# VectorE's running maximum and exponents of the last chunk, put ahead of the second residual and norm of chunk 1

## The reference, cut to what matters

```
def step(carry, kv):                      # time mixing, over 1024 positions
    num, den, mx = carry
    ck, cv = kv
    max_out = jnp.maximum(mx, ck + tf)
    e1 = jnp.exp(mx - max_out)
    e2 = jnp.exp(ck + tf - max_out)
    out = (e1 * num + e2 * cv) / (e1 * den + e2)
    max_st = jnp.maximum(mx + td, ck)
    e1s = jnp.exp(mx + td - max_st)
    e2s = jnp.exp(ck - max_st)
    return ((e1s * num + e2s * cv, e1s * den + e2s, max_st), out)
...
x = _layernorm(x + _L0_attn_ref(x, ...))      # first residual and norm
x = _layernorm(x + _L0_ffn_ref(x, ...))       # second residual and norm
x = _layernorm(x + _L1_attn_ref(x, ...))      # convolutions, gate
x = _layernorm(x + _L1_ffn_ref(x, ...))       # experts
```

## Time and profile before

| | |
|---|---|
| median of 3 runs | 439.88 us (439.57 to 440.08) |
| the profiled execution | 439.91 us, of which its span is 437.8 us |
| TensorE busy | 409.0 us (93% of the span) |
| VectorE busy | 329.8 us (75%) |
| ScalarE busy | 194.4 us (44%) |
| GpSimd busy | 34.1 us (8%) |
| mean granted clock of TensorE | 0.986 of full speed |

### The profile page before, as it was taken

One profiled execution on the slowest core, in us unless ns is written; L12 is line 12 of the kernel. 1 busy time (PEld: TensorE's weight loads), 2 busy tenths in 40 slices (PEclk: granted clock), 3 DMA queues, 4 the chain that ended last, 5 costly groups with the idle time before them and its releaser, 6 DMA issues.

```text
span 437.8 us, 4421 instructions
## 1 busy us (share of the span) xinstructions
PE 409.0 (93%) x1507; PEld 213.3 (49%) x1507; DVE 329.8 (75%) x673; ACT 194.4 (44%) x321; POOL 34.1 (8%) x48
## 2 busy tenths in 40 slices
PE   8776997989999999999999999999999999999994
PEld 3333576668956384354544443334534433443362
DVE  4899998799855995979988798697635861364475
ACT  2355667643165413546155446263054626334432
POOL 1222433111000000000000000000000000000002
PEclk9999898999999999999999999999999999999997
DMA  7300000030000000000000000000000000000001
GB/s 243 129 1 1 1 0 1 15 141 1 0 1 0 2 0 0 1 0 1 1 1 0 0 1 24 1 0 1 0 0 1 25 1 0 1 0 0 1 0 48
DMA packets 4886, 7.10 MB, mean 16 GB/s; under 512 B 1031, under 2 KB 3713, under 8 KB 4737
## 3 DMA queue, kind: packets, MB, share of 16 engines
q1 hardware_dynamic: 4031, 4.92, 3.3%
q10 hardware_dynamic: 834, 1.91, 1.2%
HBM read 5.78 MB, written 1.05 MB: 16 GB/s over the span
## 4 chain that ended last, share of the span: by engine, by line
PE 67%; DVE 23%; ACT 4%; issue 2%; DMA 1%; POOL 1%; SPq 0%; POOLq 0%; DVEq 0%; ACTq 0%
PE ring L1369 22%; PE ring L1349 7%; PE bankA L198 5%; PE ring L1364 4%; PE ring L1351 3%; PE ring L1377 2%; DVE e2v L953 2%; PE ring L1391 2%; PE ring L1384 2%; PE ring L1395 2%; PE bankA L202 2%; PE bankA L300 2%; PE timebank L300 2%; PE specbank L275 2%; PE ring L1388 2%
## 5 line engine op out<-in xcount | busy, mean ns | idle before, releaser
L1369 PE MATMUL ring<-hm,wc 128*128 128x512 f32 (+1 forms) x252 | 108.6, 580 | 0.0
L1369 PEld LDWEIGHTS ring<-hm,wc 128*128 128x128 f32 x252 | 46.1, 190 | 61.0 <-issue 52.1
L1578 DVE SCALAR_TENSOR_TENSOR hm<-xtm,cst,h 128x512 f32<-128x512 bf16 x48 | 33.2, 746 | 2.8 <-ACT h L1483 2.8
L198 PE MATMUL bankA<-wconv,h2w 128*128 128x256 f32 x128 | 32.2, 398 | 0.0
L1497 ACT ACTIVATE gts<-ring 128x512 f32<-128x512 f32 (+1 forms) x18 | 9.9, 550 | 49.0 <-PE ring L1369 49.0
L1483 ACT ACTIVATE h<-ring,vec 128x512 f32<-128x512 f32 x32 | 21.8, 687 | 18.2 <-PE ring L1351 15.7
L198 PEld LDWEIGHTS bankA<-wconv,h2w 128*128 128x128 f32 x128 | 24.0, 197 | 4.7 <-issue 1.8
L1364 PE MATMUL ring<-hm,wc 64*128 64x512 f32 (+1 forms) x84 | 22.9, 621 | 1.3 <-DVE hm L1578 1.3
L1667 DVE SCALAR_TENSOR_TENSOR f2e<-hl,f2e 128x512 f32<-128x512 f32 (+1 forms) x9 | 5.7, 632 | 24.0 <-ACT hl L1528 23.9
L1349 PE MATMUL ring<-zs,wc 128*128 128x512 f32 x40 | 20.8, 603 | 0.8 <-DVE zs L1669 0.8
L1494 ACT ACT_TABLE_LOAD x8 | 10.3, 1283 | 25.3 <-PE ring L1369 25.3
(11 more groups left out here) (280 smaller groups left out, 810.4 us busy)
## 6 DMA issues: line engine op xcount, KB each, us to landing
wc<-in_w_c SPq DMA_DIRECT2D x1, 1664.0 KB
out<-xall SPq DMA_DIRECT2D x8, 128.0 KB, 1.9
cst<-in_const ACTq DMA_DIRECT2D x1, 838.5 KB, 8.9
wc<-in_x_feat SPq DMA_DIRECT2D x1, 768.0 KB, 9.6
wc<-in_k_time ACTq DMA_DIRECT2D x1, 512.0 KB
bconv<-in_bcast SPq DMA_DIRECT2D x1, 512.0 KB, 10.3
wc<-in_x_feat ACTq DMA_DIRECT2D x1, 256.0 KB, 3.8
wa<-in_w_a SPq DMA_DIRECT2D x1, 256.0 KB, 3.7
```

The lines of the kernel that those rows point to most:

```text
L198: ins = pe.matmul(at, h2w[:, n, u % 2, u // 2:u // 2 + P], wconv[:, tap, :], start=False, stop=(h == HALVES - 1 and tap == TAPS - 1))
L1369: ins = pe.matmul(dst[:, at], wc[:, w:w + P], hm[:, seat(j, made + g - 1), at], start=False, stop=(g == PAIRS - 1))
L1578: dve.scalar_tensor_tensor(hm[:, seat(j, k), :], picked, cst[:, C_EG + g:C_EG + g + 1], h[:, g, :], ALU.is_equal, ALU.mult).then_inc(S["hm ...
```

## The change

In VectorE's function `one(c)` the call of `maxima(3)` is taken away from the start of iteration 3 and put into iteration 2, behind `output_end(2)` and ahead of `residual_end(1)`. The condition is written as `c == 2` on the iteration before. All other iterations and all other engines keep their instructions and their order, and no instruction is added or dropped.

```
                 def one(c):
-                    if valid(c):
+                    if valid(c) and not (lambda c: c == 2)(c - 1):
                         maxima(c)
                     if valid(c - 1):
                         residual_mid(c - 1)
...
                         output(c)
                         rounded(c - 1)
                         output_end(c)
+                        if c == 2:
+                            maxima(c + 1)
                         residual_end(c - 1)
```

## The result

The changed kernel takes 443.54 us (median of 16 runs, 442.75 to 445.0), the kernel before 440.38 us (median of 16 runs, 439.37 to 442.91). The ratio is 1.0070, with a 95% interval of 1.0057 to 1.0082: slower by 3.2 us between the medians. Forecast were 441.5 us and a range of 440.4 to 442.9. The direction is right, the size is half of what it should be, and the range doesn't hold it. The three runs known at the time of the prediction had a median of 439.88 us, 0.5 us lower than the later, larger sample.

A forecast was written before the change was run, and what follows sets the result against it. The prediction took ScalarE's queue to set the time between 60 and 70 us. The profiled 439.91 us plus 1.58 gave 441.49, with the median of runs 0.03 lower, so 441.5 us; range 440.4 to 442.9.

The forecast's parts named there:

- The place and the mechanism: Between 60 and 70 us ScalarE's queue sets the time; L605 waits for GpSimd's factors; earlier exponents gain nothing.
- The reason given: ScalarE takes its queue in order with L605 ahead of L629, so exponents ready at 64.3 can't be used sooner.
- The slack of 1.00 us: Chunk 1's norm factors could come 1.00 us later before L605 moved: 66.84 - 65.84.
- GpSimd's factors, 1.29 us taken between 1.29 and 2.13: GpSimd's power and product beside residual_mid(2) were bounded at 1.29 to 2.13 us; the lower end was taken.
- The direct delay of 1.58 us: L605 starts 1.58 us later: 3.35 of delay, less 1.00 of slack, less 0.77 that GpSimd saves.
- nothing absorbs it: TensorE's restart and chunk 3's VectorE chain both move by 1.58 us, and all that follows keeps its distances.
- VectorE's chain had no cover to give: Spare time lies on VectorE, not TensorE: its next statistics wait 1.91 us for TensorE at 86.07.
- The clock, put into the sum at no change: TensorE's 3.41 us at half clock behind its restart stays whole after the change, adding nothing to the sum.
- The prediction's own sign: Much less or more than 3.4 us at 0.50 in the 10 us behind TensorE's restart would show it wrong.
- It costs 3.41 / 2 = 1.7 us now: The half-clock stretch from 73.60 to 77.01, filled with matmuls, costs the kernel before 1.7 us.
- the dearer side: TensorE's low clock lasts longer or a second stretch follows its restart, costing up to another 1.7 us.
- Rival 3: TensorE's longer pause brings more low clock: 0.5 to 1.7 us on top, 442.0 to 443.2 us; chance 0.17.

The follow-up runs named there:

- late_2pow: Kernel before, with two spare GpSimd powers of 128x4 ahead of the factors of chunk 1's second norm: 443.14 us, ratio 1.0055.
- exps_first: Changed kernel, with ScalarE doing chunk 3's three exponentials (L629, L633, L635) ahead of the norm L605 in iteration 3: 441.41 us, ratio 1.0019.
- split_exps: Changed kernel, with ScalarE doing L629 ahead of L605 and L633 and L635 behind the copies h2T and h2w: 440.51 us, ratio 1.0000.
- pad_1op: Kernel before, with one spare VectorE addition of 128x512 ahead of residual_end(1): 440.76 us, ratio 1.0014.
- half_scans: Kernel before, with only the two scans L930 of maxima(3) moved ahead of residual_end(1): 440.96 us, ratio 1.0011.
- late_1pow: Kernel before, with one spare GpSimd power ahead of the factors of chunk 1's second norm: 441.32 us, ratio 1.0013.
- filled kernel of before: Kernel before, with 19 spare matmuls in TensorE's pauses of iterations 3 and 4: 440.0 us, ratio 0.9985.
- filled pair: Kernel before and changed kernel, each with the same 19 spare matmuls in iterations 3 and 4: 440.0 and 441.92 us.
- fill3_after: Changed kernel, with 14 spare matmuls in iteration 3 alone: 442.53 us, ratio 1.0042 to the kernel before.
- fill4_after: Changed kernel, with 5 spare matmuls in iteration 4 alone: 442.92 us, ratio 1.0053 to the kernel before.

## Why the prediction was wrong

- **The place and the mechanism: right.** ScalarE's queue sets the time there, L605 waits for GpSimd, and the exponents that came 2.65 us sooner were of no use behind it. late_2pow shows the cause without VectorE's move. The reason given, that L605 stands ahead of the exponentials, is true but not the whole: with the exponentials ahead (exps_first, split_exps) ScalarE took L629 at 6.54 us behind `rwkv` at the soonest, and in the kernel before the exponents were ready at 6.03.
- **The slack of 1.00 us: right.** Factors that were 0.60, 1.12, 1.26 and 2.34 us late (pad_1op, half_scans, late_1pow, late_2pow) moved L605 by 0.01, 0.11, 0.26 and 1.34 us.
- **GpSimd's factors, 1.29 us taken between 1.29 and 2.13: right.** 67.98 to 69.27 is 1.29. The power beside VectorE's statistics out of PSUM, which the trace of before didn't show, took 1.02 us. The rule of the Trainium skill (SBUF — State Buffer, "Who interferes with whom"), that a VectorE instruction with at most one SBUF input doesn't contend with GpSimd, agrees.
- **The direct delay of 1.58 us, and that nothing absorbs it: right.** 1.58 at L605, 1.58 at TensorE's restart, 1.60 over the loop at full clock, and 313.2 us behind it in both. VectorE's chain had no cover to give, as the prediction says, but also no distance: at full clock it is TensorE that waits for it (0.54 us for `xq` in the filled kernel of before).
- **The clock, put into the sum at no change: the step that failed.** The prediction took the one low stretch behind the restart of the profiled execution as the kernel's own, at a fixed place, and asked only whether that one would move or a second follow. It stands elsewhere from one execution to the next, and there is a second pause, in iteration 4, that the prediction never looked at; the profiled execution of before happened to show nothing behind it. The prediction's own sign, much more than 3.4 us at 0.50 within 10 us of the restart, doesn't show in the changed profile: the added low time stands at 91.9 us. What the runs show in its place is about 3.4 us more of low clock on average over four executions each, worth about 1.2 us: 1.24 by the medians with and without spare matmuls, 1.2 by the table.
- **"It costs 3.41 / 2 = 1.7 us now": too large for the kernel before.** One stretch behind iteration 3 cost 64.32 - 63.80 = 0.52 us there, since VectorE's chain is close behind TensorE's and bounds next. Behind iteration 4 the stretches cost more: 6.83 us there and none in iteration 3 cost 65.80 - 63.80 = 2.00 us in the kernel before, and in the changed one 10.2 us in both places cost 67.74 - 65.40 = 2.34 to 68.55 - 65.40 = 3.15 us.
- **Rival 3 was the case that came** (chance 0.17), at 442.0 to 443.2; the time is 0.3 us above it. Its upper end allowed for one more stretch only, and the range was cut at 442.9. Measured from the base that the later runs gave, its 2.1 to 3.3 us of slowdown hold the 3.16.
- **The base.** 440.38 instead of 439.88 is a quarter of the miss: 440.38 + 1.58 = 441.96, and 1.58 us remain. The clock is shown for about 1.2 of them; the other 0.3 to 0.4 us are not accounted for, and are about the difference between the medians of the filled pair (1.92) and their traces (1.60).
- The rule of the Trainium skill (TensorE: Matmul & The Clock Gate, "HAM oscillation — how this bites in real kernels"), that work which restarts behind a longer wait starts at the lower clock, spoke for the dearer side. The traces don't contradict it, but are too few to confirm it: with the pause at 3.17 us four of four executions had a low stretch at the restart or soon behind it, with 2.49 us three of four, and there it began 0.6 to 1.6 us behind the restart. The clock term that the sum lacked rests on the table above, not on the rule.

What stays open: there are four traced executions of each kernel, so the 1.2 us of clock from them carries the uncertainty of stretches of 3.4 us; why the change brings more low clock is argued from the longer pause and not shown; and whether the low stretches behind iteration 4 are more frequent after the change, or only as frequent (the last part of its pause is 1.4 us in both), isn't settled. By fill3_after filling the longer pause takes something away; by fill4_after perhaps the other as well.

## What to carry to other kernels

Measure the distance from a common event on both sides of the change, not from the start of the span: the 1.58 us were exact, while the spans differed by 5.1. When a change lengthens a pause of TensorE, price the clock as a term of the sum with a size of its own, and look at every pause near it, also where the one profile at hand shows full clock. And before work is brought forward on one engine, look at when its reader is free, not only at what stands ahead in its queue: ScalarE was free for L629 6.54 us behind `rwkv` at the soonest, and the old order had the exponents ready at 6.03.

## What the runs showed of the hardware

Between 10 and 140 us TensorE's stretches at half the clock lasted 3.4 or 6.8 us in every trace here, at places that differ from execution to execution of the same kernel: from none to 6.8 us behind one pause of 1.40 us that four short transposes precede. The four traced executions of the kernel before have spans of 437.8 to 440.2 us, and all of that spread lies ahead of the transposes of the second part, where the stretches stand; behind them each takes 313.1 to 313.2 us. What a stretch costs depends on where it stands: 3.41 us of it cost 0.5 us where VectorE's chain was close behind, and 6.83 us cost 2.0 us one iteration later.
